# Scan and gate constants loaded in the norm and made in the preparation, first image's gate inputs prefetched in the scan, first chunk issued from two queues

## The reference, cut to what matters

```python
    def _L1_conv_ref(x, in_proj_w, conv_w, conv_b, x_proj_w, dt_projs_w, dt_projs_b, A_logs, Ds, out_norm_g, out_norm_b, out_proj_w):
        ...
        As = -jnp.exp(A_logs).reshape(K, DI, N)
        out_y = selective_scan(xs, dts, As, Bs, Cs, Ds.reshape(K, DI))
        inv_y = jnp.flip(out_y[:, 2:4], -1)
        wh_y = jnp.transpose(out_y[:, 1].reshape(B, DI, W, H), (0, 1, 3, 2)).reshape(B, DI, L)
        invwh_y = jnp.transpose(inv_y[:, 1].reshape(B, DI, W, H), (0, 1, 3, 2)).reshape(B, DI, L)
        y = out_y[:, 0] + inv_y[:, 0] + wh_y + invwh_y
        ...
        mu = y.mean(-1, keepdims=True)
        var = y.var(-1, keepdims=True)
        y = (y - mu) / jnp.sqrt(var + 1e-05) * out_norm_g + out_norm_b
        y = y * jax.nn.silu(z)
        return y @ out_proj_w.T
```

## Time and profile before

| | us |
|---|---|
| median of 3 runs | 4348.4 (4346.66 to 4348.88) |
| the profiled execution, device time | 4336.19 |
| its span | 4334.2 |
| TensorE busy | 3358.8 (77%) |
| VectorE busy | 3519.2 (81%) |
| ScalarE busy | 2716.3 (63%) |
| GpSimd busy | 1596.2 (37%) |
| granted TensorE clock, mean | 0.859 |

### The profile page before, as it was taken

One profiled execution on the slowest core, in us unless ns is written; L12 is line 12 of the kernel. 1 busy time (PEld: TensorE's weight loads), 2 busy tenths in 40 slices (PEclk: granted clock), 3 DMA queues, 4 the chain that ended last, 5 costly groups with the idle time before them and its releaser, 6 DMA issues. The chain is left out here.

```text
span 4334.2 us, 110093 instructions
## 1 busy us (share of the span) xinstructions
PE 3358.8 (77%) x46784; PEld 1676.5 (39%) x46784; DVE 3519.2 (81%) x3560; ACT 2716.3 (63%) x4416; POOL 1596.2 (37%) x1151
## 2 busy tenths in 40 slices
PE   6788873168777766317877876868999999999998
PEld 4477631012222123101222222553566565565663
DVE  5555467989999957789999995768988888888882
ACT  2366538744555534864555553443899999999995
POOL 0122210089999951009999994000000000000000
PEclk9799986577889887657788887887999999999999
DMA  5343203432223210352222221351221222222211
GB/s 130 83 70 74 54 12 104 148 77 74 70 72 79 63 42 8 112 147 74 74 64 75 78 58 39 104 168 48 56 56 56 64 56 56 64 56 56 55 41 49
DMA packets 160558, 309.95 MB, mean 72 GB/s; under 512 B 69591, under 2 KB 105751, under 8 KB 156100
## 3 DMA queue, kind: packets, MB, share of 16 engines
q1 hardware_dynamic: 160068, 302.91, 26.7%
HBM read 194.44 MB, written 107.83 MB: 70 GB/s over the span
## 5 line engine op out<-in xcount | busy, mean ns | idle before, releaser
L2275 DVE TENSOR_REDUCE l3a_mx<-l3a_mx 128x2 f32<-128x768 f32 x1296 | 1165.3, 952 | 162.4 <-PE l3a_mx L2174 158.3
L2241 ACT ACTIVATE l3a_p<-l3a_s 128x384 f32<-128x384 f32 x2592 | 1181.1, 492 | 115.1 <-PE l3a_s L2188 107.0
L1490 POOL TENSOR_TENSOR l_scan_sc<-l_scan_s,l_scan_repc 128x768 f32<-128x768 f32 x576 | 1035.9, 1858 | 6.4 <-DVE l_scan_s L1468 6.0
L1427 ACT ACTIVATE l_scan_da<-l_scan_da,l_scan_a 128x768 f32<-128x768 f32 x576 | 504.0, 875 | 630.2 <-PE l_scan_da L1350 630.2
L2188 PE MATMUL l3a_s<-l3a_q,l3a_k 125*32 125x384 f16 x10368 | 803.2, 327 | 5.5 <-DMA l3a_q<-l3a_m 3.6
L2174 PE MATMUL l3a_mx<-l3a_k,l3a_q 124*32 124x384 f16 x10368 | 673.2, 335 | 62.3 <-DMA l3a_q<-l_qx 35.4
L1350 PE MATMUL l_scan_dup<-l_scan_du,l_scan_pick 96*128 96x512 bf16 (+1 forms) x1152 | 345.7, 389 | 317.8 <-DMA l_scan_dt<-l_dtp 159.5
L2200 PE MATMUL l3a_o<-l3a_p,l3a_vh 128*32 128x288 f32 x6912 | 569.1, 405 | 0.8 <-issue 0.4
L1481 POOL TENSOR_TENSOR l_scan_bup<-l_scan_dus,l_scan_repb 128x768 f32<-128x768 f32 x192 | 356.4, 1856 | 484.5 <-DMA l_scan_repc<-l_bcp 484.5
L2142 POOL TENSOR_TENSOR l3a_norm<-l3a_out,l3a_spread 128x576 f32<-128x576 f32 x24 | 34.4, 1435 | 1344.7 <-DMA l3a_spread<-l_inverses 1344.7
L1350 PE MATMUL l_scan_da<-l_scan_dt,l_scan_pick 96*128 96x512 bf16 (+1 forms) x1152 | 338.8, 382 | 157.4 <-DVE l_scan_s L1468 155.2
(11 more groups left out here) (203 smaller groups left out, 4259.2 us busy)
## 6 DMA issues: line engine op xcount, KB each, us to landing
l3a_q<-l_qx SPq DMA_DIRECT2D x96, 486.0 KB
l_scan_du<-l_dup SPq DMA_DIRECT2D x144, 144.0 KB, 2.8
l_scan_dt<-l_dtp SPq DMA_DIRECT2D x144, 144.0 KB, 3.3
l_scan_repb<-l_bcp SPq DMA_DIRECT2D x48, 384.0 KB
l_scan_repc<-l_bcp SPq DMA_DIRECT2D x48, 384.0 KB
l_dtp<-l_prep_high_t SPq DMA_DIRECT2D x16, 432.0 KB, 3.2
l_dup<-l_prep_high_u SPq DMA_DIRECT2D x16, 432.0 KB, 3.2
l_dtp<-l_prep_middle_t SPq DMA_DIRECT2D x16, 432.0 KB, 3.2
```

Source lines behind the costliest of these rows:

```text
L1427: act.activation(da_ps[st % 2][:, 0:TC], da_ps[st % 2][:, 0:TC], ACT.Exp, scale=A[:, column:column + 1]).then_inc(exped, 1)
L1490: pool.tensor_tensor(SC[:, st % NSC, :], S[:, n, :], REPC[k % 2][:], ALU.mult).then_inc(weighted, 1)
L2241: act.activation(P[:, k % NP, third * SW:(third + 1) * SW], s_ps[u % NS_PS][:, 0:SW], ACT.Exp)\
L2275: dve.tensor_reduce(MX[:, qt % (NB * KT), 2 * pair:2 * pair + 2], mx_ps[n % NR][:, :, 0:RG], AX_X, ALU.max)\
```

## The change: what it does

- `LateConstants` holds A, PICK, SUM, the gate's D, g, b and weights. SP issues their seven loads in the norm of the same layer. DVE and ACT turn them into what is used (A, eps, `centre`, `centre_skip`) at the start of the preparation. The scan and the gate no longer load or make them.
- The first chunk of a scan is issued from two queues: SP issues DU and REPB, ACT issues DT and REPC. The second chunk follows on SP.
- `GateInputs` holds U, z, y and yt of image 0 only. They are loaded in the scan, in chunks 2, 6, 12 and 14, in place of GU and GZ of both images. Image 1's U, y, yt and z are loaded at the start of the gate.
- YS and the semaphores of its stores outlive the scan: SP waits for the last stores in the gate, behind the load of image 1's U, and no longer at the scan's end.
- Each layer has one scope with semaphores more (`pre + "k"`), so one clearing and barrier more at its end.

```diff
@@ ssm_prepare @@
             def _(act):
+                act.wait_ge(late.a_capped, 1)
+                act.activation(late.A[:], late.A[:], ACT.Exp).then_inc(late.a_exped, 1)
                 act.wait_ge(folded, 1)
...
                 dve.memset(bias[DI:128, :], 0.0).then_inc(placed, 1)
+                late.make(dve)
                 dve.wait_ge(loaded, 64)
...
+class LateConstants:
...
+    def load(self, sp):
+        t, pre = self.t, self.pre
+        for dst, src in ((self.A, t[pre + "A"]), (self.Dk, t[pre + "D"]), (self.g, t[pre + "norm_g"]),
+                         (self.bb, t[pre + "norm_b"]), (self.w_sb, t[pre + "owT"]), (self.PICK, t["pick"]),
+                         (self.SUM, t["state_sum"])):
+            sp.dma_start(dst[:], src).then_inc(self.loaded, 16)
+
+    def make(self, dve):
+        dve.wait_ge(self.loaded, 16 * 7)
+        dve.tensor_scalar(self.A[:], self.A[:], 88.0, None, ALU.min).then_inc(self.a_capped, 1)
+        dve.memset(self.eps[:], 1e-5).then_inc(self.centre_made, 1)
+        dve.tensor_tensor(self.centre[:], self.eye[0:DI, 0:DI], self.ones_mean[:], ALU.subtract)\
+           .then_inc(self.centre_made, 1)
+        dve.tensor_reduce(self.dsum[:], self.Dk[:], AX_X, ALU.add).then_inc(self.centre_made, 1)
+        dve.wait_ge(self.centre_made, 3)
+        dve.tensor_scalar(self.centre_skip[:], self.centre[:], self.dsum[:, 0:1], None, ALU.mult)\
+           .then_inc(self.centre_made, 1)
+        dve.wait_ge(self.a_exped, 1)
+        dve.tensor_scalar(self.A[:], self.A[:], A_MOST, -1.0, ALU.min, ALU.mult).then_inc(self.a_turned, 1)
+        dve.wait_ge(self.centre_made, 4)
+        dve.wait_ge(self.a_turned, 1)
...
@@ ssm_scan @@
-                load_chunk(0)
+                load_first()
                 load_chunk(1)
                 for k in range(CHUNKS):
                     if k + 2 < CHUNKS:
                         load_chunk(k + 2)
                     if place(k * NN)[2]:
                         store_y(k)
-                    if k % 4 == 2 and k // 4 < len(gate_loads):
-                        gate_loads[k // 4](sp)
-                for x in y_stored:
-                    sp.wait_ge(x, 16 * CHUNKS // 4)
+                    if k == 2:
+                        sp.dma_start(gate.U0[:], u_dram[0]).then_inc(gate.u_loaded, 16)
+                    if k == 6:
+                        sp.dma_start(gate.Z0[:], z_dram[0]).then_inc(gate.u_loaded, 16)
+                    if k == CHUNKS // 2:
+                        for x in y_stored:
+                            sp.wait_ge(x, 16 * CHUNKS // 8)
+                        sp.dma_start(gate.Y0[:], y_dram[1]).then_inc(gate.y_loaded, 16)
+                    if k == CHUNKS // 2 + 2:
+                        sp.dma_start(gate.YT0[:], y_dram[2]).then_inc(gate.y_loaded, 16)
...
@@ ssm_gate @@
-                for b in range(B):
-                    for dst, src in ((y, y_dram[2 * b + 1]), (yt, y_dram[2 * b + 2])):
-                        sp.dma_start(dst[:, b, :], src).then_inc(loaded[b], 16)
+                sp.dma_start(U[1][:], u_dram[1]).then_inc(u_loaded, 16)
+                for x in gate_in.y_stored:
+                    sp.wait_ge(x, 16 * 3 * B)
+                sp.dma_start(y[1][:], y_dram[3]).then_inc(y_loaded, 16)
+                sp.dma_start(yt[1][:], y_dram[4]).then_inc(y_loaded, 16)
+                sp.dma_start(Z[1][:], z_dram[1]).then_inc(z_loaded, 16)
...
-                    if n % PER == 0:
-                        pool.wait_ge(loaded[b], 32)
+                    if n == 0:
+                        pool.wait_ge(gate_in.y_loaded, 32)
+                    if n == PER:
+                        pool.wait_ge(y_loaded, 32)
```

More of the change, by code:

```diff
@@ L1225, in ssm_scan, with __init__ @@
+class GateInputs:
+    def __init__(self, nc, s):
+        self.U0, self.Z0, self.Y0, self.YT0 = (s.sb(n, [DI, L]) for n in ("u0", "z0", "y0", "yt0"))
+        self.YS = s.sb("ys", [DI, 2, 768])
+        self.u_loaded, self.y_loaded = s.sem("u_loaded"), s.sem("y_loaded")
+        self.y_stored = [s.sem(f"y_stored{i}") for i in range(2)]
+def ssm_scan(nc, name, t, pre, late, gate, eye, dt_dram, du_dram, bc_dram, u_dram, z_dram, y_dram):
     NG, NT = 4, 3
@@ L1237, in ssm_scan @@
     with Scope(nc, name) as s:
-        PICK = s.sb("pick", [DI, NG, 128], BF16)
-        SUM = s.sb("sum", [128, NG, 32])
-        A = s.sb("a", [128, ND * NN])
+        PICK, SUM, A, YS, y_stored = late.PICK, late.SUM, late.A, gate.YS, gate.y_stored
         DT = [s.sb(f"dt{i}", [DI, NT, TC], BF16) for i in range(2)]
@@ L1262, in ssm_scan @@
             s.sem(n) for n in ("scanned", "weighted", "piece_summed", "y_taken"))
-        y_stored = [s.sem(f"y_stored{i}") for i in range(2)]
         BANKS = [(0, CH), (CH, TC - CH)]
@@ L1298, in _, with load_first @@
             def _(sp):
-                sp.dma_start(PICK[:], t["pick"]).then_inc(consts, 16)
-                sp.dma_start(SUM[:], t["state_sum"]).then_inc(consts, 16)
-                sp.dma_start(A[:], t[pre + "A"]).then_inc(consts, 16)
+                def load_first():
+                    for part in range(3):
+                        sp.dma_start(DU[0][32 * part:32 * part + 32, :, :],
+                                     du_dram[0, part, :, span(0)].rearrange("(t e) l -> e t l", t=NT))\
+                          .then_inc(loaded[0], 16)
+                    sp.dma_start(REPB[0][:], bc_dram[0, :, span(0)].unsqueeze(0).to_broadcast([8, NS, TC]))\
+                      .then_inc(rep_loaded[0], 16)
                 def load_chunk(k):
@@ L1399, in _ @@
             def _(act):
-                act.wait_ge(a_capped, 1)
-                act.activation(A[:], A[:], ACT.Exp).then_inc(a_exped, 1)
-                act.wait_ge(a_turned, 1)
+                for part in range(3):
+                    act.dma_start(DT[0][32 * part:32 * part + 32, :, :],
+                                  dt_dram[0, part, :, span(0)].rearrange("(t e) l -> e t l", t=NT))\
+                       .then_inc(loaded[0], 16)
+                act.dma_start(REPC[0][:], bc_dram[1, :, span(0)].unsqueeze(0).to_broadcast([8, NS, TC]))\
+                   .then_inc(rep_loaded[0], 16)
                 def take_y(k):
@@ L1507, in ssm_gate @@
     with Scope(nc, name) as s:
-        y = s.sb("y", [DI, B, L])
-        yt = s.sb("yt", [DI, B, L])
-        yc = s.sb("yc", [DI, B, L])
-        YG = s.sb("yg", [DI, B, L])
-        w_sb = s.sb("w", [DI, C])
-        g = s.sb("g", [DI, 1])
-        bb = s.sb("b", [DI, 1])
-        eps = s.sb("eps", [DI, 1])
-        Dk = s.sb("dk", [DI, ND])
-        dsum = s.sb("dsum", [DI, 1])
-        centre = s.sb("centre", [DI, DI])
-        centre_skip = s.sb("centre_skip", [DI, DI])
+        y = [gate_in.Y0, s.sb("y1", [DI, L])]
+        yt = [gate_in.YT0, s.sb("yt1", [DI, L])]
+        U = [gate_in.U0, s.sb("u1", [DI, L])]
+        Z = [gate_in.Z0, s.sb("z1", [DI, L])]
+        yc = [s.sb(f"yc{b}", [DI, L]) for b in range(B)]
+        YG = [s.sb(f"yg{b}", [DI, L]) for b in range(B)]
+        w_sb, g, bb, eps = late.w_sb, late.g, late.bb, late.eps
+        centre, centre_skip = late.centre, late.centre_skip
         acc = [s.ps(f"acc{i}", [DI, CH]) for i in range(NA)]
@@ L1522, in ssm_gate @@
         out_ps = [s.ps(f"out{i}", [CP, CH]) for i in range(NO)]
-        loaded = [s.sem(f"loaded{b}") for b in range(B)]
-        consts, centre_made = s.sem("consts"), s.sem("centre_made")
+        u_loaded, y_loaded, z_loaded = s.sem("u_loaded"), s.sem("y_loaded"), s.sem("z_loaded")
         joined, centred, kept, squared, varied, logged, rooted, scaled, done = (
```

81 lines of the change are left out of this document (39 added, 42 removed).

## The result

| | before | after | difference |
|---|---|---|---|
| median of 9 runs each, us | 4341.84 | 4320.17 | ratio 0.9937, 95% interval 0.9924 to 0.995 |
| profiled execution, us (span) | 4336.19 (4334.2) | 4323.98 (4322.2) | -12.2 |
| norm of layer 1 to norm of layer 3, profiled, us | 2151.64 | 2125.33 | -26.3 |

What follows compares the result with a forecast made beforehand. Stages follow one another behind barriers, and VectorE bounds the scan proper; the change acts at the scan's and gate's starts. 31.3 + 4.0 - 0.8 = 34.5 us off 4348.4 gave 4313.9 us, range 4306 to 4325.

Steps and rivals of the forecast that it cites:

- gate, two layers: Gate's start in layers 1 and 2: the seventh copy comes 15.7 and 15.6 us earlier, together 31.3 us.
- scan's start: From t, SP's first issue in the scan, to VectorE's first product: 2.0 us less a layer, 4.0 us for two.
- new scope: End of layers 1 and 2: a third scope to clear adds 0.4 us a layer, 0.8 us in all.
- the cover in the preparation: Preparation: six small moved instructions, at most 1.6 us, fit in VectorE's 2.76 us wait for the stage's weights.
- The gate begins at s + 1.35: Scan's end: with s the issue of its last store, the gate begins after 0.30 us issue and 1.05 us barrier.
- yt of image 1 at s + 16.7: Gate's loads: yt of image 1 lands 16.7 us after s, the middle of 15.6 and 17.8.
- The seventh copy at s + 19.7: Gate: VectorE's copy for image 1's first job comes 19.7 us after s, instead of 35.40 in layer 1.
- The rival of the second chunk that overtakes REPC: Scan's start: REPC, alone in ACT's queue, competes with SP's loads; VectorE starts near t + 14.3, total 4317.9 us; chance 0.12.
- Preparation and norm at no cost: Norm and preparation: SP's seven new issues, some 3 us, and the six moved instructions are covered; cost none.
- The steps of the scan stretch: Scan: other tile addresses lengthen each of 576 steps; 60 ns uses up the gain, 90 ns gives 4365.7 us; chance 0.03.

## Why the prediction came out as it did

| term, us | forecast | by stages |
|---|---|---|
| gate, two layers | -31.3 | -14.70 - 13.67 = -28.4 |
| scan's start | -4.0 | +0.08 - 0.40 = -0.3 |
| new scope | +0.8 | +0.43 + 0.36 = +0.8 |
| all other stages of layers 1 and 2 | 0 | +1.6 |
| sum | -34.5 | -26.3 |

The time came out inside the range and 7.1 us above the forecast. The gate's mechanism, the scope and the cover in the preparation held as reasoned. The scan's start did not, but as a term of 4.0 us in 34.5 it was too small to push the time out of the range.

*The gate begins at s + 1.35.* Right: s + 1.22, and the run with the store's wait put back gives the 2.3 us of the step.

*yt of image 1 at s + 16.7.* Right: 15.68 and 16.65 (14.56 to 17.73 over the sixteen unchanged gates).

*The seventh copy at s + 19.7.* The mechanism was right and the size off. I let the chain be as long as before or, by the clock, up to 2.9 us shorter; it was 1.1 and 2.0 us longer: 19.48 and 20.38 us from GpSimd's start to the copy against 18.38. Of that 1.1 us lie ahead of the first scaling in both layers, and 0.9 in layer 2 is that scaling itself, 1.47 us long. I read the mean clock of the old stretch, 0.84, and not where in it the low part lay. Before, the clock was at the lower level from GpSimd's start on, for 5.8 us in layer 1 and 6.5 in layer 2, and then rose; now the clock, which had risen at the scan's end, fell 1.5 us into the gate, for 6 us. The extra matmuls show that what TensorE does in the pause decides it, and that a low stretch costs the chain 1.7 to 3.4 us (17.30 to 18.99 against 15.60 or 15.61 in all six gates with extra matmuls). But the old chain paid for one as well, and this profile lies at the long end. On the mean of the sixteen gates the chain to the first scaling is only 0.4 us longer than the 17.85 of before (18.19 in layer 2), and the first scaling, 1.15 us in place of 0.61, is the larger part. That second part is the neighbour: GpSimd's additions for image 1 ended at 1594.51 + 6.91 = 1601.42, ahead of the first scaling, and now they lie beside it. The run without U shows this too. On the mean of the sixteen gates the copy stood at s + 20.58, which is 0.9 us a layer over the forecast, 1.8 of the 34.5 us.

*Scan's start, 2.0 us a layer.* This step failed. It said that three issues fewer and a second queue bring the data earlier, and that REPB and REPC would follow at their former pace. TensorE's first matmul stood where it had (t + 6.88, 6.99 before), although all issues came 1.3 us earlier and from two queues, and REPC took what was left. The one-queue run had that matmul at t + 6.42 and 6.08: by these two starts the constants' issues were worth 0.6 to 1.1 us to DU and DT, and the second queue, which starts REPB and REPC beside them, seems to have taken it back. The reckoning had a slip as well: it has DU and DT in at t + 5.1, 3.85 us behind t + 1.26, while the old rows have TensorE's first matmul 5.69 us behind DU's first issue (867.94 to 873.63). By them alone it was t + 5.7. The rival of the second chunk that overtakes REPC forecast the number, t + 14.3, by a mechanism that the one-queue run takes away: ahead of the second chunk in the same queue, REPC is no earlier. What the runs show in its place is two facts together. The REP loads run on half of the DMA engines, and those of the second chunk on the same half at the same time: all four had been issued by 882.02, and the share was 0.53 to 0.56 from 887.79 to 893.79, not 1. Remove either (all engines: t + 10.1; second chunk held: t + 11.6) and the start moves by 4.4 or 2.9 us. Whether an engine takes turns between queues, the rule of the Trainium skill that I weighed ("DMA: Bandwidth & Descriptors", section "Queues, rings and completion order"), these runs leave open; it isn't what decided. I had the row, DMA at 0.47 with a load outstanding, and took it for the pace of such a load instead of asking which engines stood idle. Whether the constants' 1.30 us would have shown without the second queue stays open, by the spread told above.

*Preparation and norm at no cost.* Right for the cover: the six instructions ended at 682.13, and VectorE's copy still waited 2.10 us for the weights (2.76 before). But the preparation and the stages ahead of it were 0.2 to 0.3 us longer each in both layers. In the preparation most of it lies ahead of that copy, which stood 3.01 and 3.10 us behind VectorE's first instruction (2.83 and 2.82 before): the weights came that much later. Why they did, and what lengthened the stages ahead, stays open. With 0.2 us a layer in the gate behind the copy and 0.37 in layer 2's scan they make the 1.6 us of the table.

*The scope, 0.4 us a layer.* Right. *The steps of the scan stretch:* they did not; product to s is 689.07 and 688.90 against 689.24 and 688.53.

## What to carry to other kernels

When a wait of a DMA remains and the DMA engines are busy to a half, look at how the load is spread before adding queues or issuing earlier: here the order of two dimensions in a broadcast load was worth 4.4 us a layer, and the second queue and the earlier issue together nothing that shows. When a change closes a gap, TensorE's clock and the neighbours of each instruction come from another phase than in the old trace: take the bounds from windows, not from a mean, look at several executions (the same chain took 17.30 to 18.99 us), and ask which engine's work will now lie beside which. Measure a stage by its own marks when untouched stages spread by more than the edit is worth.
